# The product in three layer norms of a two-layer gated cross-attention block, made on VectorE instead of GpSimd

## The chip, the cores and the metric

The kernel runs on one core of one Trainium2 chip. The metric is the device time of one execution in microseconds (us), lower is better. It is given as the median of several executions.

## What is computed

The input `x` has 32 batches of 256 tokens with 256 features; `ctx` has 77 tokens for each batch. Two layers follow each other, each with a cross-attention and a feed-forward part. Each of the four parts begins with a layer norm and is added to the stream with a gate:

```
def _layernorm(x, axis=-1, eps=1e-05):
    m = jnp.mean(x, axis=axis, keepdims=True)
    v = jnp.var(x, axis=axis, keepdims=True)
    return (x - m) / jnp.sqrt(v + eps)

x = x + tanh(g_xattn[0]) * L0_xattn(_layernorm(x), ctx, ctx, mask, ...)   # relu attention        norm 0
x = x + tanh(g_ffn[0])   * L0_ffn(_layernorm(x), k0, k1, k2, s0, s1, s2)  # 256-1024-1024-256     norm 1
x = x + tanh(g_xattn[1]) * L1_xattn(_layernorm(x), ctx, Wq, Wkv, Wc)      # argmax, 16 heads      norm 2
x = x + tanh(g_ffn[1])   * L1_ffn(_layernorm(x), ...)                     # 64 experts, top 8     norm 3
```

## The kernel before

Everything is done batch by batch, and the engines run their instructions in an order that is written out by hand, one list for each engine, with semaphores between them. One round of the loop, `body(n)`, works on several batches at once: the second attention and the shared expert of batch c = n - 1, the first feed-forward of batch n, the first attention of batch m = n + 1, and GpSimd's scatters of batches n - 2 and n - 3. The round has two halves, `first(n)` and `second(n)`. Norms 1, 2 and 3 (the 2nd to 4th norm) lie in `second(n)`. Each core engine takes its own list strictly in order, so an instruction that waits holds all that stand behind it on its engine. After the 32 batches come the 64 experts, which the change does not touch.

A norm passes over four engines. VectorE makes the new stream tile (`a_x1`, L1529; `b_x2`, L1548; `c_x3`, L1618), its statistics (`ln_sums`, L1490) and from them `nt`, which holds the variance with EPS and the negated mean (`ln_moments`, L1502 and L1503, semaphore `ln_st`). GpSimd's `ln_coef(i, b)` makes the root `rs` = (variance + EPS) to the power -0.5 (L590) and the product `nb` = negated mean times `rs` (L592), and reports `ln_cf`. ScalarE's `ln_norm` (L726) waits for `ln_cf` and makes x * rs + nb. TensorE turns the result over (`transposes`, L986), ScalarE and VectorE take it out of PSUM in two halves (`tr_high`, L731; `tr_low`, L1512). Norm 0 is different: GpSimd normalises it itself (L601).

In `second(n)` the order on VectorE is: `c_x3` and the moments of norm 3, `b_l1(3)` (L1534), `a_x1` and the moments of norm 1, `tr_low(3)`, `b_x2` and the moments of norm 2, `d_gu(0)` (L1684 and L1686), `tr_low(1)`, `d_gu(1)`. On TensorE it is: half of the feed-forward's last product (`b_l2`, L1069), the transposes of norm 3, the other half, `d_gu(0)`, the transposes of norm 1, `d_gu(1)`, `d_route`, `d_gu(2)`, the transposes of norm 2. On GpSimd it is: `keep_x1` (L585), `ln_coef(3)`, a scatter, `ln_coef(1)`, two scatters, `ln_coef(2)`. A scatter is an indirect DMA issued by GpSimd (L574).

```
            def ln_norm(i, b, src, dst):              # ScalarE
                act.wait_ge(ln_cf[i], b + 1)
```

Of the kernel before, what the change touches and what calls it, by code (L numbers as in the profile page):

```python
# [13 lines left out]
ALU = mybir.AluOpType  # L14
# [78 lines left out]
def build(nc, x, ctxT, maskT, g_xattn, g_ffn, wq0, wk0, wv0, bq0, bk0, bv0, k0, k1, k2, s0, s1, s2,  # L93
          wqT1, wkvT1, wcT1, gates_w, sgu_w, sdown_w, egu_w, edown_w, out, xrows, table):
    es = ExitStack()
    with es:
        def sb(name, shape, dt=F32):
            return es.enter_context(nc.sbuf_tensor(name, shape, dt))
# [4 lines left out]
        def sems(name, n):  # L103
            return [sem(f"{name}{i}") for i in range(n)]
# [19 lines left out]
        def two(ap):  # L124
            return ap[:, :].rearrange("p (a n) -> p a n", a=2)
# [56 lines left out]
        nt = [sb(f"nt{i}", [P, 2, T2]) for i in range(4)]  # L182
        rs = [sb(f"rs{i}", [P, T2]) for i in range(4)]
        nb = [sb(f"nb{i}", [P, T2]) for i in range(4)]
# [95 lines left out]
        ln_st, ln_root, ln_cf, ln_nm, ln_dve = (sems(n, 4) for n in ("ln_st", "ln_root", "ln_cf", "ln_nm", "ln_dve"))  # L280
# [48 lines left out]
        def on(b):  # L329

            return not isinstance(b, int) or 0 <= b < NB
# [134 lines left out]
        def _(pool):  # L466
            g = nc.gpsimd
# [119 lines left out]
            def ln_coef(i, b):  # L587

                pool.wait_ge(ln_st[i], b + 1)
                g.tensor_tensor(rs[i][:, :], nt[i][:, 0, :], minushalf[:, :], ALU.pow).then_inc(ln_root[i], 1)  # L590
                pool.wait_ge(ln_root[i], b + 1)
                g.tensor_tensor(nb[i][:, :], nt[i][:, 1, :], rs[i][:, :], ALU.mult).then_inc(ln_cf[i], 1)  # L592

            def ln_norm(b):

# [8 lines left out]
            def body(n):  # L604
# [22 lines left out]
                if on(c):  # L627
                    ln_coef(3, c)
                if on(d):
                    scatter(d, 'c')  # L630
                if on(m):
                    ln_coef(1, m)
# [784 lines left out]
        def _(dve):  # L1417
            v = nc.vector
            ln_chain = [Steps(dve, ln_dve[i], 2) for i in range(4)]

            def plain(site):

                v.memset(dve_pad[:, site:site + 1], 0.0)
# [59 lines left out]
            def ln_sums(i, b, src, made, each=1):  # L1483


                w(dve, ln_nm[i], b)
                dve.wait_ge(made, each * b + each)
                ln_chain[i].start(b)
                for t in range(T2):
                    last = v.bn_stats(stats[i][:, t, :], src[:, t, :])  # L1490
                ln_chain[i].did(last)

            def ln_moments(i):

                ch = ln_chain[i]
                ch.wait()
                plain(8 + i)
                for t in range(T2):
                    last = v.bn_aggr(mv[i][:, t, :], stats[i][:, t, :])
                ch.did(last)  # L1500
                ch.wait()
                v.tensor_scalar(nt[i][:, 1, :], mv[i][:, :, 0], -1.0, None, ALU.mult)  # L1502
                v.tensor_scalar(nt[i][:, 0, :], mv[i][:, :, 1], EPS, None, ALU.add).then_inc(ln_st[i], 1)  # L1503
                ch.end()

            def ln_first(b):
                ln_sums(0, b, x0, x_in, 16)
                ln_moments(0)

            def tr_low(i, b, lo, hi):  # L1510
                dve.wait_ge(tr_hi[i], b + 1)
                v.tensor_tensor(lo[:, :, :], two(ps_turned[i]), hi[:, :, :], ALU.subtract).then_inc(tr_lo[i], 1)  # L1512


            def a_v(b):
                dve.wait_ge(v_rdy, b + 1)
                w(dve, vr_ev, b)
                v.scalar_tensor_tensor(v32[:, :], ps_pt0[0:S2, 0:D], 1 / WS, bv[0:S2, :], ALU.mult, ALU.add).then_inc(v_ev, 1)

            def a_l(b):  # L1520
                dve.wait_ge(s_ev, b + 1)
                w(dve, sv_rdy, b)
                v.tensor_tensor(l32[:, :], s32[:, :], mT[:, :], ALU.add).then_inc(l_ok, 1)

            def a_x1(b):
                dve.wait_ge(sv_ev, b + 1)
                w(dve, x1_copied, b)
                w(dve, ln_nm[1], b)
                v.scalar_tensor_tensor(x1[:, :, :], o32[:, :, :], G0X, x0[:, :, :], ALU.mult, ALU.add).then_inc(x1_ok, 1)  # L1529


            def b_lo(hi, lo, hh, hl, j, b):
                dve.wait_ge(hi.sem, hi.nth(j, b))
                v.scalar_tensor_tensor(hl[:, 2 * j:2 * j + 2, :], two(bank[j % 2]), 0.0, hh[:, 2 * j:2 * j + 2, :],  # L1534
                                       ALU.max, ALU.subtract).then_inc(lo.sem, 1)
# [4 lines left out]
            def b_l1(j, b):  # L1540
                b_lo(l1_hi, l1_lo, h1_h, h1_l, j, b)

            def b_x2(b):
                dve.wait_ge(l2_rdy, b + 1)
                dve.wait_ge(x1_copied, b + 1)
                w(dve, x3_ok, b)
                w(dve, ln_nm[2], b)
                v.scalar_tensor_tensor(x2[:, :, :], two(ps_yo), F0, x1_kept[:, :, :], ALU.mult, ALU.add).then_inc(x2_ok, 1)  # L1548
# [57 lines left out]
            def c_norm(r, b):  # L1606
                t, c = divmod(r, C2)
                dve.wait_ge(av_rdy.sem, av_rdy.nth(r, b))
                av = ps_m[:, 0:HC * VW].rearrange("p (h n) -> p h n", n=VW)
                v.reciprocal(rden[:, :], av[:, :, DH]).then_inc(av_dve, 1)  # L1610
                dve.wait_ge(av_dve, 5 * b + r + 2)
                v.tensor_tensor(att[:, t, c * P:(c + 1) * P].rearrange("p (h n) -> p h n", n=DH), av[:, :, 0:DH],
                                rden[:, :].unsqueeze(2).to_broadcast([P, HC, DH]), ALU.mult).then_inc(av_ev.sem, 1)

            def c_x3(b):
                dve.wait_ge(wc_rdy, b + 1)
                w(dve, x4_ok, b)
                v.scalar_tensor_tensor(x3[:, :, :], two(ps_m), G1X, x2[:, :, :], ALU.mult, ALU.add).then_inc(x3_ok, 1)  # L1618
# [61 lines left out]
            def d_gu(j, b):  # L1680

                dve.wait_ge(gu_th.sem, gu_th.nth(j, b))
                two_ = two(bank[j % 2])
                v.scalar_tensor_tensor(ga[:, j, :], th[:, j, :], 1.0, two_[:, 0, :], ALU.add, ALU.mult).then_inc(gu_dve, 1)  # L1684
                dve.wait_ge(gu_dve, 4 * b + j + 1)
                v.scalar_tensor_tensor(ac[:, j, :], ga[:, j, :], 0.5 / (WS * WS), two_[:, 1, :], ALU.mult, ALU.mult).then_inc(gu_ac.sem, 1)  # L1686

            def d_ac(j, b):
                dve.wait_ge(ac_hi.sem, ac_hi.nth(j, b))
                v.tensor_tensor(ac_l[:, j, :], ac[:, j, :], ac_h[:, j, :], ALU.subtract).then_inc(ac_lo.sem, 1)  # L1690
# [11 lines left out]
            def first(n):  # L1702
# [28 lines left out]
                if on(m) and on(n):  # L1731
                    ln_first(m)
# [28 lines left out]
            def second(n):  # L1761
                m, c = n + 1, n - 1
                if on(c):
                    c_norm(3, c)
                if on(n):
                    b_l1(1, n)
                if on(m):
                    a_v(m)
                if on(n):
                    b_l1(2, n)  # L1770
                if on(m):
                    a_l(m)
                if on(c):
                    tr_low(4, c, at_l, at_h)
                    c_x3(c)
                    ln_sums(3, c, x3, x3_ok)
                    ln_moments(3)
                if on(n):
                    b_l1(3, n)
                if on(m):  # L1780
                    a_x1(m)
                    ln_sums(1, m, x1, x1_ok)
                    ln_moments(1)
                if on(c):
                    tr_low(3, c, xt_l[3], xt_h[3])
                if on(n):
                    b_x2(n)
                    ln_sums(2, n, x2, x2_ok)
                    ln_moments(2)
                if on(c):  # L1790
                    d_gu(0, c)
                if on(m):
                    tr_low(1, m, xt_l[1], xt_h[1])
                if on(c):
                    d_gu(1, c)
                    d_gu(2, c)
                    d_ac(0, c)
# [5 lines left out]
            def last_batch(b):  # L1803
                c_norm(3, b)
                tr_low(4, b, at_l, at_h)
                c_x3(b)
                ln_sums(3, b, x3, x3_ok)
                ln_moments(3)
                tr_low(3, b, xt_l[3], xt_h[3])
                d_max(b)  # L1810
                d_gu(0, b)
                d_choose(b)
                d_gu(1, b)
                d_pos(b)
                d_slots(b)
                d_ac(0, b)
                d_ac(1, b)
                d_gu(2, b)
                d_gu(3, b)
                d_ac(2, b)  # L1820
                d_ac(3, b)
                d_x4(b)
# [124 lines left out]
```

## Time and profile before

| what | value |
|---|---|
| median of 3 runs | 1972.29 us (1964.68 to 1974.4) |
| time of the profiled execution | 1962.54 us |
| its span, first to last instruction | 1960.8 us |
| TensorE busy | 1706.9 us, 87% of the span |
| VectorE busy | 1329.0 us, 68% |
| GpSimd busy | 1068.3 us, 54% |
| ScalarE busy | 971.5 us, 50% |

The profile is of one execution. PE is TensorE's matmuls, DVE is VectorE, ACT is ScalarE, POOL is GpSimd. L592 is line 592 of the kernel. A row of the timeline gives the start, the duration, the engine, the line, the operation, the output and the inputs, and in brackets how long the engine had been idle and whose work ended that. Two VectorE rows can overlap by some tens of nanoseconds, since the next instruction starts before the last one's result is written. A transpose is a matmul on TensorE and appears as one.

### The profile page before, as it was taken

What the parts mean: (1) busy time and instruction counts of PE and PEld (TensorE: products, weight loads), DVE (VectorE), ACT (ScalarE), POOL (GpSimd) and SP (SyncE); (2) the same over time, 40 slices, a digit from 0 to 9 for tenths busy, and PEclk for the clock granted to TensorE, in tenths of its full rate; (3) what the DMA queues carried; (4) which work ended last, traced back from release to release, by engine and by line L of the source; (5) the groups of instructions that cost most, each with busy time, mean ns of one, the idle gap of its engine ahead of it and who ended that gap; (6) DMA issues with size and microseconds to landing.
All of it is one profiled execution on the core that took longest, in us unless ns stands there. A gap on an engine that the chain in (4) does not pass through costs nothing.

```text
span 1960.8 us, 51981 instructions
## 1 busy us (share of the span) xinstructions
PE 1706.9 (87%) x17309; PEld 1427.6 (73%) x17309; DVE 1329.0 (68%) x4615; ACT 971.5 (50%) x2803; POOL 1068.3 (54%) x1772
## 2 busy tenths in 40 slices
PE   3799999989899998999999999999999986457665
PEld 2687887878788887788878888888888864246554
DVE  5477777767677776677777777777777764335564
ACT  2365555555455554555555555555555543123332
POOL 2115555555455555555555555555555543568897
PEclk8899999999999999999999999999999997678999
DMA  4001100000000101000000000000000000147887
GB/s 126 8 14 21 21 19 19 19 14 19 19 19 19 19 19 19 19 19 19 17 16 19 19 19 19 19 19 19 19 19 19 18 13 13 45 124 186 199 205 154
DMA packets 97568, 80.15 MB, mean 41 GB/s; under 512 B 33835, under 2 KB 95224, under 8 KB 97528
## 3 DMA queue, kind: packets, MB, share of 16 engines
q1 hardware_dynamic: 68856, 60.46, 11.2%
q0 software_dynamic: 28672, 19.18, 5.5%
q8 instruction: 22, 0.36, 0.1%
q14 instruction: 18, 0.15, 0.0%
HBM read 51.63 MB, written 27.95 MB: 41 GB/s over the span
## 4 chain that ended last, share of the span: by engine, by line
PE 55%; issue 15%; DVE 14%; ACT 7%; POOL 4%; DMA 3%; another core or an unknown queue 1%; POOLq 0%; SPq 0%; DVEq 0%; ACTq 0%
PE bank L1055 15%; PE bank L964 7%; PE ps_m L964 5%; ACT p L787 3%; PE ps_lg L1113 3%; PE ps_yo L1069 3%; PE ps_lg L964 3%; PE ps_tr L986 3%; PE ps_yo L964 3%; PE ps_pt L1128 2%; PE bank L1041 2%; DMA xg<-xrows,gid 2%; PE ps_pt L964 1%; DVE rmax L1599 1%; PE ps_lg L1020 1%
## 5 line engine op out<-in xcount | busy, mean ns | idle before, releaser
L574 POOL DMA_INDIRECT table<-toki,slot x512 | 520.2, 1016 | 242.5 <-issue 196.3
L518 POOL TENSOR_TENSOR pool_pad<-pad_in 128x1 f32<-128x1 f32 x456 | 115.7, 254 | 400.8 <-PE ps_lg L1113 176.6
L787 ACT ACTIVATE p<-ps_lg,rmax 128x77 f32<-128x77 f32 x1024 | 235.6, 349 | 146.8 <-DVE rmax L1599 141.6
L1055 PE MATMUL bank<-h_h,wb 128*128 128x256 f16 x2048 | 266.3, 273 | 4.3 <-issue 2.2
L1055 PE MATMUL bank<-h_l,wb 128*128 128x256 f16 x2048 | 266.3, 273 | 0.0
L1055 PEld LDWEIGHTS bank<-h_l,wb 128*128 128x128 f16 x2048 | 200.8, 98 | 23.8 <-issue 0.2
L1055 PEld LDWEIGHTS bank<-h_h,wb 128*128 128x128 f16 x2048 | 193.2, 98 | 28.3 <-issue 2.8
L590 POOL TENSOR_TENSOR rs<-nt,minushalf 128x2 f32<-128x2 f32 x128 | 92.6, 724 | 188.2 <-DVE nt L1503 176.7
L1534 DVE SCALAR_TENSOR_TENSOR h_l<-bank,h_h 128x512 f16<-128x512 f32 x256 | 174.8, 683 | 12.0 <-ACT h_h L768 6.7
L1599 DVE TENSOR_REDUCE rmax<-ps_lg 128x8 f32<-128x616 f32 x128 | 101.6, 794 | 84.9 <-PE ps_lg L1113 84.8
L773 ACT ACTIVATE h_h<-bank 128x512 f16<-128x512 f32 x128 | 76.9, 601 | 124.3 <-PE bank L1055 124.3
L1512 DVE TENSOR_TENSOR xt_l<-ps_tr,xt_h 128x512 f16<-128x512 f32 x128 | 88.0, 687 | 62.9 <-ACT xt_h L731 52.3
L1069 PE MATMUL ps_yo<-wb,h_h 128*128 128x256 f16 x512 | 116.7, 275 | 0.1
L1069 PE MATMUL ps_yo<-wb,h_l 128*128 128x256 f16 x512 | 116.5, 274 | 0.0
L768 ACT ACTIVATE h_h<-bank 128x512 f16<-128x512 f32 x128 | 76.2, 597 | 80.6 <-PE bank L1041 44.3
L1604 DVE TENSOR_TENSOR pt_l<-ps_pt,pt_h 128x384 f16<-128x384 f32 x128 | 70.4, 550 | 65.7 <-ACT pt_h L793 65.5
L793 ACT ACTIVATE pt_h<-ps_pt 128x384 f16<-128x384 f32 x128 | 62.9, 491 | 103.4 <-PE ps_pt L1128 100.4
L680 POOL DMA_INDIRECT out<-ey,aid x64 | 101.5, 1586 | 18.6 <-POOL pool_pad L518 7.0
L964 PE MATMUL bank<-xt_h,gu_h 128*128 128x256 f16 x512 | 99.8, 277 | 10.6 <-DVE ac L1686 9.4
L1041 PE MATMUL bank<-xt_h,wb 128*128 128x256 f16 x512 | 100.0, 278 | 10.1 <-DVE dn_l L1438 5.9
L731 ACT ACTIVATE xt_h<-ps_tr 128x512 f16<-128x512 f32 x128 | 76.4, 597 | 60.2 <-PE ps_tr L986 53.0
L1490 DVE BATCH_NORM_STATS2 stats<-x 128x6 f32<-128x256 f32 x256 | 96.0, 417 | 13.4 <-DMA x<-in_x 3.7
(287 smaller groups left out, 4691.6 us busy)
## 6 DMA issues: line engine op xcount, KB each, us to landing
ew<-in_egu_w SPq DMA_DIRECT2D x64, 256.0 KB
xrows<-xr SPq DMA_DIRECT2D x32, 320.0 KB
x<-in_x SPq DMA_DIRECT2D x32, 256.0 KB
out<-x SPq DMA_DIRECT2D x32, 256.0 KB
table<-toki,slot POOLq DMA_INDIRECT x512
ew<-in_edown_w SPq DMA_DIRECT2D x64, 128.0 KB
ctx<-in_ctxT SPq DMA_DIRECT2D x32, 77.0 KB, 2.0
stage_b<-in_k SPq DMA_DIRECT2D x1, 1024.0 KB, 8.0
```

The source lines that it names most:

```text
L518: return g.tensor_tensor(pool_pad[:, site:site + 1], pad_in[:, :], pad_in[:, :], ALU.mult)
L574: g.indirect_dma_start(out=table, out_offset=bass.IndirectOffsetOnAxis(ap=slot[:, t, k:k + 1], axis=0), in_=toki[:, t:t + 1], in_offset=No ...
L590: g.tensor_tensor(rs[i][:, :], nt[i][:, 0, :], minushalf[:, :], ALU.pow).then_inc(ln_root[i], 1)
L680: g.indirect_dma_start(out=out, out_offset=bass.IndirectOffsetOnAxis(ap=aid[u][:, 0:1], axis=0), in_=ey[u][:, :], in_offset=None, bounds_c ...
L787: ins = a.activation(p32[:, h * S2:(h + 1) * S2], ps_lg[:, h // HB, h % HB * S2:(h % HB + 1) * S2], ACT.Exp, bias=rmax[r % 2][:, h:h + 1])
L964: ins = mm(out_, s_, m_, start=(start and i == 0), stop=(stop and i == len(seq) - 1))
L1041: ins = mm(two(bank[j % 2])[:, m % 2, :], s_, m_, start=(k == 0), stop=(k == 3))
L1055: ins = mm(two(bank[j % 2])[:, m % 2, :], wb1[:, k, m * P:(m + 1) * P], hp[:, k, :], start=(i == 0 and k == 0), stop=(i == 1 and k == FK - 1))
L1069: ins = mm(two(ps_yo)[:, t, :], hp[:, k, t * P:(t + 1) * P], wb2[:, k, :], start=(i == 0 and k == 0), stop=(i == 1 and k == FK - 1))
L1490: last = v.bn_stats(stats[i][:, t, :], src[:, t, :])
L1534: v.scalar_tensor_tensor(hl[:, 2 * j:2 * j + 2, :], two(bank[j % 2]), 0.0, hh[:, 2 * j:2 * j + 2, :], ALU.max, ALU.subtract).then_inc(lo.s ...
L1599: v.tensor_reduce(rmax[r % 2][:, :].rearrange("p (g h) -> p g h", g=2), lg, AX, ALU.max, negate=True).then_inc(z_ok.sem, 1)
```

## The change

For norms 1, 2 and 3 GpSimd makes only the root. A new VectorE function, `ln_shift`, waits for the root and makes the product. It stands one piece of work after the norm's moments: for norm 3 behind `b_l1(3)`, for norm 1 behind `tr_low(3)`, for norm 2 behind `d_gu(0)`. In the last batch it stands right behind the moments. Norm 0 stays on GpSimd.

```diff
@@ GpSimd, ln_coef
                 g.tensor_tensor(rs[i][:, :], nt[i][:, 0, :], minushalf[:, :], ALU.pow).then_inc(ln_root[i], 1)
-                pool.wait_ge(ln_root[i], b + 1)
-                g.tensor_tensor(nb[i][:, :], nt[i][:, 1, :], rs[i][:, :], ALU.mult).then_inc(ln_cf[i], 1)
+                if i == 0:
+                    pool.wait_ge(ln_root[i], b + 1)
+                    g.tensor_tensor(nb[i][:, :], nt[i][:, 1, :], rs[i][:, :], ALU.mult).then_inc(ln_cf[i], 1)
@@ VectorE
+            def ln_shift(i, b):
+                dve.wait_ge(ln_root[i], b + 1)
+                v.tensor_tensor(nb[i][:, :], nt[i][:, 1, :], rs[i][:, :], ALU.mult).then_inc(ln_cf[i], 1)
@@ VectorE, second(n)
                 if on(n):
                     b_l1(3, n)
+                if on(c):
+                    ln_shift(3, c)
                 if on(m):
                     a_x1(m)
                     ln_sums(1, m, x1, x1_ok)
                     ln_moments(1)
                 if on(c):
                     tr_low(3, c, xt_l[3], xt_h[3])
+                if on(m):
+                    ln_shift(1, m)
                 if on(n):
                     b_x2(n)
                     ln_sums(2, n, x2, x2_ok)
                     ln_moments(2)
                 if on(c):
                     d_gu(0, c)
+                if on(n):
+                    ln_shift(2, n)
                 if on(m):
                     tr_low(1, m, xt_l[1], xt_h[1])
@@ VectorE, last_batch(b)
                 ln_moments(3)
+                ln_shift(3, b)
                 tr_low(3, b, xt_l[3], xt_h[3])
```

## Rows read from the trace of the kernel before

**Rows 1.** The page: span, TensorE's busy time, its granted clock in 40 slices.

```profile
span 1960.8 us, 51981 instructions
PEclk8899999999999999999999999999999997678999
```

**Rows 2.** What TensorE waited for: us in total, times, longest.

```profile
PE ps_tr L986 <- ACT xr L726: 34.9, 25, 6.7
...
PE ps_tr L986 <- issue: 6.5, 6, 1.1
```

**Rows 3.** The chain that ended last, norm 3 of one batch: start, us.

```profile
828.28 0.73 POOL rs L590
...
829.09 0.58 POOL nb L592
...
829.78 1.10 ACT xr L726 x2
...
831.01 0.63 PE ps_tr L986 x4
```

**Rows 4.** Timeline of GpSimd, the same batch.

```profile
829.83 1.05 POOL L574 DMA_INDIRECT table<-toki,slot  x1 [0.17 <-issue]
831.12 0.72 POOL L590 TENSOR_TENSOR rs<-nt,minushalf 128x2 f32<-128x2 f32 x1 [0.24 <-DVE nt L1503]
...
835.67 0.72 POOL L590 TENSOR_TENSOR rs<-nt,minushalf 128x2 f32<-128x2 f32 x1 [0.73 <-DVE nt L1503]
```

**Rows 5.** Timeline of VectorE, the same batch.

```profile
828.11 0.68 DVE L1534 SCALAR_TENSOR_TENSOR h_l<-bank,h_h 128x512 f16<-128x512 f32 x1
828.86 0.75 DVE L1529 SCALAR_TENSOR_TENSOR x<-o,sc,x 128x512 f32<-128x512 f32 x1
...
830.86 0.16 DVE L1503 TENSOR_SCALAR nt<-mv 128x2 f32<-128x2 f32 x1
832.31 0.69 DVE L1512 TENSOR_TENSOR xt_l<-ps_tr,xt_h 128x512 f16<-128x512 f32 x1 [1.28 <-ACT xt_h L731]
833.42 0.75 DVE L1548 SCALAR_TENSOR_TENSOR x<-ps_yo,sc,x_kept 128x512 f32<-128x512 f32 x1 [0.43 <-PE ps_yo L1069]
...
835.94 0.42 DVE L1686 SCALAR_TENSOR_TENSOR ac<-ga,bank 128x256 f32<-128x256 f32 x1
```

**Rows 6.** Timeline of ScalarE, the same batch.

```profile
831.68 0.60 ACT L731 ACTIVATE xt_h<-ps_tr 128x512 f16<-128x512 f32 x1 [0.81 <-PE ps_tr L986]
832.17 1.08 ACT L726 ACTIVATE xn<-x,nb,rs 128x256 f32<-128x256 f32 x2
...
836.99 1.08 ACT L726 ACTIVATE xn<-x,nb,rs 128x256 f32<-128x256 f32 x2
```

**Rows 7.** Timeline of TensorE, the same batch: the transposes of norm 1.

```profile
834.53 0.60 PE L986 MATMUL ps_tr<-ident,xn 128*128 128x128 f32 x4
```

**Rows 8.** All products of GpSimd: durations min/median/max, then its group's busy us and mean ns.

```profile
L592 POOL TENSOR_TENSOR nb<-nt,rs x128: 193/196/609, 8.2 to 1681.0; 128x2 f32<-128x2 f32 x128
...
L592 POOL TENSOR_TENSOR nb<-nt,rs 128x2 f32<-128x2 f32 x128 | 35.4, 276 | 10.0
```

**Rows 9.** Groups of VectorE, by form.

```profile
L1588 DVE TENSOR_TENSOR vc<-vc 77x16 f16<-77x16 f32 x32 | 5.6, 175 | 1.1
...
L1668 DVE TENSOR_TENSOR val<-key,kept 128x128 f32<-128x128 f32 x32 | 9.4, 292 | 1.1
```

**Rows 10.** Timeline of GpSimd and VectorE, where VectorE waited for GpSimd.

```profile
523.90 0.62 POOL L585 COPY x_kept<-x 128x512 f32<-128x512 f32 x1
...
524.62 0.75 DVE L1529 SCALAR_TENSOR_TENSOR x<-o,sc,x 128x512 f32<-128x512 f32 x1 [5.78 <-POOL x_kept L585]
```

**Rows 11.** Timeline: a VectorE instruction with two SBUF inputs beside a scatter.

```profile
838.91 0.99 POOL L574 DMA_INDIRECT table<-toki,slot  x1 [0.45 <-issue]
...
839.37 0.42 DVE L1690 TENSOR_TENSOR ac_l<-ac,ac_h 128x256 f16<-128x256 f32 x1
```

**Rows 12.** Timeline of TensorE, norm 1 of a batch in which GpSimd's root came late.

```profile
1230.69 0.52 PE L986 MATMUL ps_tr<-ident,xn 128*128 128x128 f32 x3 [1.22 <-ACT xn L726]
```

## The prediction

> **What bounds the kernel now.** I read the page first: the span is 1960.8 us [rows 1], TensorE is busy in 87% of it (the table above), and its granted clock stands at 9 tenths or more of full speed in nearly every slice until the experts begin [rows 1]. So in the loop over the batches TensorE sets the pace, and the question is what keeps it idle there. The list of waits answers that. The longest wait of TensorE inside the loop is for `xr`, the output of norm 3, in front of the transposes of L986: 25 waits with 34.9 us, and six more of the same size whose releaser is given as issue, with 6.5 us [rows 2]. Without the longest (6.7 us, in a disturbed batch) and one of 4.6 us in the last batch, this is (34.9 - 6.7 - 4.6 + 6.5) / 29 = 1.04 us each. Batch by batch in the timeline it is nearly always 1.07 or 1.08 us. A batch takes 49.05 us from one `c_x3` to the next where nothing disturbs it, so this wait is 2% of the batch and the only gap of that size in it.
>
> Next I followed the chain of the last work through norm 3 of one batch [rows 3]. GpSimd's root runs from 828.28 for 0.73 us, to 829.01. The product starts at 829.09 and takes 0.58 us there. ScalarE starts at 829.78, and TensorE's transposes start at 831.01. All of it is on the path. The reader should see two things. From the end of the root to ScalarE's start 829.78 - 829.01 = 0.77 us go by. And the product of two numbers per partition takes far longer here than elsewhere: the median of all 128 is 196 ns [rows 8]. The group's busy time gives how often that happens: (35.4 - 128 x 0.196) / 0.39 = 26 products of about 0.59 us [rows 8], and the timeline shows that they are the ones of norm 3 in 26 of the 32 batches. In those batches VectorE's `a_x1` starts at 828.86 and runs until 829.61 [rows 5], and the product ends 0.05 us after it. In the batches where no `a_x1` runs beside the product it takes 0.20 us.
>
> **What the change does, part by part.** *Norm 3.* Removed from the path are the step from root to product (0.08), the product (0.58) and the step to ScalarE (0.11): 0.77 us [rows 3]. Put there are three terms. The step from GpSimd to VectorE: where VectorE did wait for GpSimd, `x_kept` ended at 523.90 + 0.62 = 524.52 and VectorE started at 524.62 [rows 10], so 0.10. The product on VectorE: the trace of before has none of this form. The nearest is a tensor_tensor of 16 elements with 0.175 us, and one of 128 elements takes 0.292 [rows 9]; I take 0.17, as it has only two elements. The step from VectorE to ScalarE: L1686 ended at 836.36 and ScalarE's next dependent instruction started at 836.40, so 0.04 (L1686 in [rows 5], ScalarE in the timeline). Sum 0.31, gain 0.77 - 0.31 = 0.46 us for each batch with a long product. Bounds: with 0.08, 0.15 and 0.03 for the terms the gain is 0.51; with 0.12, 0.29 and 0.05 it is 0.31.
>
> The wait is 1.07 us, so it stays above zero (0.61) and the gain is not cut off there. ScalarE is free: it had been idle for 0.95 us in front of this instruction.
>
> VectorE pays for it. It is free of `b_l1(3)` at 828.79 [rows 5] and now stands until 829.11. The product is followed by the next instruction 0.08 us after its start, as the two writers of `nt` are, so `a_x1` starts at about 829.19 instead of 828.86: 0.33 us later. What is queued behind the waiting instruction is `a_x1`, the moments of norm 1 and `tr_low(3)`. The moments ended at 831.02 and end at 831.35; VectorE then was idle for 1.28 us in front of `tr_low(3)` [rows 5]. That idle time hides the delay. `tr_low(3)` itself comes 0.46 us earlier with the transposes, at 831.85, still behind 831.35.
>
> *Norm 1.* Its product now stands behind `tr_low(3)`. The root is there by 831.35 + 0.10 + 0.72 = 832.17 (its length in [rows 4]). The product can start when `tr_low(3)` lets it, 831.85 + 0.61 = 832.46, so it doesn't wait. ScalarE starts `xn` at 832.46 + 0.17 + 0.04 = 832.67, against 832.17 before [rows 6], so 0.50 later. It ends at 833.75, and TensorE can have it at 833.88 with the same 0.13 as in [rows 3]. TensorE comes to these transposes at 834.53 [rows 7] minus 0.46, at 834.07. So 0.19 us are to spare, where it was 834.53 - 833.38 = 1.15. This cushion is thin: it is a fixed chain of 3.33 us behind the start of the transposes of norm 3 against 3.52 us of TensorE's own work (831.01 to 834.53). If the product takes 0.12 us more and waits for the end of `tr_low(3)`, nothing is left, and what is above that is lost in every batch.
>
> *Norm 2.* Its moments and its root are 0.46 us earlier with `b_x2`, which starts when TensorE lets it (VectorE idle 0.43 in front [rows 5]). GpSimd's root ends at 835.67 + 0.72 - 0.46 = 835.93 [rows 4]. GpSimd was idle for 0.73 us in front of it, so its two scatters don't hold it. VectorE is done with `d_gu(0)` at 836.36 - 0.46 = 835.90 [rows 5], waits until 836.03, and `nb` is there at 836.20. ScalarE takes up `xn` at 836.99 - 0.46 = 836.53, held by its own earlier work. So this product costs nothing and gives nothing. It delays `tr_low(1)` by some 0.3 us; the cover is the distance of 1.2 us to the transposes of norm 2, which need that buffer. Without the cover they would be 0.3 later.
>
> *GpSimd.* It has three instructions and waits less in each batch and issues the same scatters. It is idle in front of these roots, so its shorter list is worth nothing in itself. No queue of DMAs is passed over: no DMA moves.
>
> *Sum.* 26 batches by 0.46 = 12.0 us. In the other batches with a wait, and in the first and last ones, only a product of 0.20 us is replaced: (0.08 + 0.20 + 0.11) - 0.31 = 0.08, for some six of them 0.5 us. Everything behind the transposes of norm 3 (the next `c_x3` too) moves with them, as TensorE has no other gap of this size. Together -12.5 us: the profiled execution would be 1962.5 - 12.5 = 1950.0. Its own time is 9.8 us below the median of the runs, since some batches take 1 to 8 us more in any run. Against the median it is 1972.3 - 12.5 = 1959.8 us, or -0.63%.
>
> **A rule against the trace.** In the new order `a_x1`, which reads two SBUF tiles, starts at about 829.19, and GpSimd's scatter starts 0.17 us after it is free [rows 4], at 829.18. The row shows what such a pair did: the scatter of 838.91 with 0.99 us was under way when VectorE's L1690, with two SBUF inputs, started at 839.37, and this took its usual 0.42 us [rows 11]. So I cost `a_x1` at its 0.75 us. The Trainium skill (SBUF: State Buffer, section "SBUF: two separate sides") says that VectorE and GpSimd share a pair of ports with an exclusive lock, which a VectorE instruction with two SBUF inputs takes against a GpSimd instruction, and that the loser is blocked until the other has ended. By that rule the product of 0.58 us beside `a_x1` is a blocked one, and the trace agrees (0.196 where none runs beside it). By that rule a scatter that is first would hold `a_x1` too; [rows 11] speak against it, and what it would cost is the second rival below.
>
> **The rivals.** *The cushion of norm 1 gives way* (chance 0.14). If the step or the product is longer, the gain at norm 3 is 0.31, and the product at norm 1 eats a further 0.1 to 0.2. 26 x 0.15 = 4 us are left: 1968. For it: 0.19 us is little. Against it: all steps in it are read from rows.
>
> *The scatter holds `a_x1`* (0.06), the case on the other side. The place is 829.18, and it decides when the scatter is first. Its length is 1.05 us [rows 4], so `a_x1` starts 1.04 us later than forecast, the moments of norm 1 end at 831.35 + 1.04 = 832.39, the root at 833.21, the product at 833.21 + 0.10 + 0.17 = 833.48, ScalarE at 833.48 + 0.04 + 1.08 = 834.60, and TensorE starts at 834.73 instead of 834.53. Each batch is 0.20 longer, 26 x 0.20 = +5: 1977.
>
> *GpSimd's lateness reaches VectorE* (0.08). VectorE now waits for GpSimd three times a batch, with the whole stream queued behind. One batch shows what a late root costs: TensorE stood 1.22 us in front of norm 1 [rows 12], and that batch took 50.67 instead of 49.05. If it came in each of the 26 batches it would be +42 us; in a third of them +14, which takes back the gain: about 1974, and up to 2000. It decides from where GpSimd comes to norm 3 later by more than the 2.1 us for which it now stands idle in front of that root. Against it: only two of 30 batches show it, and the change takes work from GpSimd.
>
> *More than forecast* (0.05): the late batches become rarer too, 1954.
>
> **How the numbers follow.** The forecast has 0.67, the rivals 0.14, 0.06, 0.08 and 0.05. The three runs of before span 10 us, so a median of a few may be off by 3 to 4 us, and 0.5% (9.9 us), about what a measurement of this kernel can tell from no change, lies only 2.6 us from the forecast. Of the forecast's 0.67 I put 0.53 below 1962.4 and 0.14 above; with the last rival faster has 0.57. Within 0.5% are 0.14 of the forecast, 0.13 of the first rival, the second and some of the third, 0.36. Slower is 0.07. The likeliest case alone gives 1954 to 1966. The range reaches to the lower bound of 26 x 0.51 with a fast median, 1951, and above to the rivals at 1968 and 1974: 1975.
>
> **What would show it.** Norm 3's transposes wait 0.6 us instead of 1.07. The product on VectorE takes 0.17 us and starts 0.10 behind the root. `a_x1` starts 1.0 us after the moments of norm 3 instead of 0.66 and still takes 0.75. ScalarE's `xn` of norm 1 starts 0.5 us later and TensorE doesn't wait for it. A batch takes 48.6 us. I am wrong if TensorE waits in front of norm 1, if `a_x1` is longer, or if VectorE waits for GpSimd for more than 0.4 us in many batches.

## The result, and the profile after

The changed kernel took 1944.88 us, the median of four runs (1937.5 to 1945.69). The kernel before took 1968.49 us in four runs of the same time (1963.35 to 1974.4). The ratio is 0.9871, with a 95% interval of 0.9829 to 0.9912: 1.3% faster. The forecast was 1959.8 us, or 0.63% faster, with a range from 1951 to 1975, so the direction was right, the size half of what came, and the time lies below the range. The profiled execution took 1945.69 us with a span of 1944.0 us, against 1962.54 and 1960.8 before.

First the same view as in [rows 2], what TensorE waited for. Most lines have moved down by one, so L726 is L727 now and L986 is L987; those behind the moments on VectorE have moved by five (`b_l1` is L1539, `a_x1` L1534, `tr_low` L1517, `c_x3` L1623), and the product stands at L1509.

```profile
PE ps_tr L987 <- ACT xr L727: 23.0, 20, 7.1
...
PE ps_tr L987 <- issue: 6.0, 10, 0.6
```

The wait in front of norm 3's transposes was 34.9 + 6.5 = 41.4 us for 31 waits and is 23.0 + 6.0 = 29.0 for 30: 12.4 us less. Next the chain that ended last, through norm 3 of one undisturbed batch (start, us), beside [rows 3].

```profile
1412.00 0.73 POOL rs L590
...
1412.76 0.17 DVE nb L1509
...
1413.04 1.10 ACT xr L727 x2
...
1414.28 0.63 PE ps_tr L987 x4
```

From the end of the root to ScalarE's start it is 1413.04 - 1412.73 = 0.31 us, where it was 0.77. The timelines of the same batch follow, VectorE first, then GpSimd, ScalarE and TensorE (idle time in front of an instruction, with its releaser, in brackets).

```profile
1409.75 0.75 DVE L1623 SCALAR_TENSOR_TENSOR x<-ps_m,sc,x 128x512 f32<-128x512 f32 x1 [2.15 <-PE ps_m L965]
...
1411.83 0.68 DVE L1539 SCALAR_TENSOR_TENSOR h_l<-bank,h_h 128x512 f16<-128x512 f32 x1
1412.76 0.16 DVE L1509 TENSOR_TENSOR nb<-nt,rs 128x2 f32<-128x2 f32 x1 [0.25 <-POOL rs L590]
1412.88 0.76 DVE L1534 SCALAR_TENSOR_TENSOR x<-o,sc,x 128x512 f32<-128x512 f32 x1
...
1415.57 0.69 DVE L1517 TENSOR_TENSOR xt_l<-ps_tr,xt_h 128x512 f16<-128x512 f32 x1 [0.52 <-ACT xt_h L732]
1416.18 0.15 DVE L1509 TENSOR_TENSOR nb<-nt,rs 128x2 f32<-128x2 f32 x1
```

```profile
1412.92 1.05 POOL L574 DMA_INDIRECT table<-toki,slot  x1 [0.19 <-issue]
```

```profile
1413.04 1.09 ACT L727 ACTIVATE xr<-x,nb,rs 128x256 f32<-128x256 f32 x2 [0.49 <-DVE nb L1509]
...
1416.37 1.09 ACT L727 ACTIVATE xn<-x,nb,rs 128x256 f32<-128x256 f32 x2 [0.83 <-issue]
```

```profile
1408.92 0.38 PE L965 MATMUL ps_m<-wc_h,at_l 128*128 128x256 f16 x2
...
1414.28 0.63 PE L987 MATMUL ps_tr<-ident,xr 128*128 128x128 f32 x4 [0.61 <-ACT xr L727]
...
1417.80 0.60 PE L987 MATMUL ps_tr<-ident,xn 128*128 128x128 f32 x4
```

The reader should see that TensorE stands 0.61 us where it stood 1.07, that the product takes 0.16 us on VectorE, and that `a_x1` behind it takes its usual 0.76. TensorE doesn't wait in front of norm 1's transposes. An undisturbed batch, from one set of norm 3's transposes to the next, is 48.56 us where it was 49.05. Two things remain to be explained. The wait in front of norm 3 is 12.4 us shorter, but the time fell by 23.6. And before the experiments nothing said which of the product's two costs, its own length on GpSimd or `a_x1` beside it, had been in the way.

### The profile page after: what moved, and what is told of

Read it like the earlier page. It is cut to its first block, busy times and chain, and to the rows that moved or that the text cites. A ratio compares the mean times of both kernels' runs of the same rounds, so it can differ in the third digit from the quotient of the medians.

```text
span 1944.0 us, 51981 instructions
## 1 busy us (share of the span) xinstructions
PE 1708.6 (88%) x17309; PEld 1425.7 (73%) x17309; DVE 1340.3 (69%) x4711; ACT 974.4 (50%) x2803; POOL 1038.4 (53%) x1676
## 4 chain that ended last, share of the span: by engine, by line
PE 47%; issue 21%; DVE 13%; ACT 8%; POOL 7%; DMA 2%; another core or an unknown queue 1%; POOLq 1%; SPq 0%; DVEq 0%; ACTq 0%
PE bank L1056 13%; PE bank L965 8%; ACT p L788 4%; PE ps_yo L1070 3%; PE ps_lg L1114 3%; PE ps_tr L987 3%; PE ps_m L965 3%; PE ps_yo L965 3%; PE ps_pt L1129 2%; POOL table L574 2%; PE bank L1042 2%; POOL pool_pad L518 2%; DVE rmax L1604 2%; DVE pt_l L1609 1%; PE ps_lg L965 1%
## 5 line engine op out<-in xcount | busy, mean ns | idle before, releaser
L1056 PEld LDWEIGHTS bank<-h_h,wb 128*128 128x128 f16 x2048 | 193.4, 98 | 28.5 <-issue 2.9
L1539 DVE SCALAR_TENSOR_TENSOR h_l<-bank,h_h 128x512 f16<-128x512 f32 x256 | 175.0, 684 | 15.5 <-ACT h_h L769 10.6
L1517 DVE TENSOR_TENSOR xt_l<-ps_tr,xt_h 128x512 f16<-128x512 f32 x128 | 88.1, 688 | 35.8 <-ACT xt_h L732 28.6
```

What stands on the lines that cost most here:

```text
L1056: ins = mm(two(bank[j % 2])[:, m % 2, :], wb1[:, k, m * P:(m + 1) * P], hp[:, k, :], start=(i == 0 and k == 0), stop=(i == 1 and k == FK - 1))
```

## The experiments

There are four groups of kernels, and those of a group ran on one chip, together with the kernel before. The chips of the groups turned out not to be alike. Ratios are to the kernel before on the same chip, with 95% intervals. "Batch" is the time of an undisturbed batch.

### The two halves, and the wait alone

Four kernels: the change again, its norm 3 alone, its norms 1 and 2 alone, and the kernel before with `a_x1` held until GpSimd's product is done.

```diff
@@ r2_norm3, r3_norms12: which products stay on GpSimd (ln_shift only for the others)
-                if i == 0:
+                if i != 3:            # r2_norm3
+                if i in (0, 3):       # r3_norms12
@@ r4_alone: the kernel before, VectorE
                 if on(m):
+                    if on(c):
+                        dve.wait_ge(ln_cf[3], c + 1)
                     a_x1(m)
```

> The changed kernel once more, with more rounds. Theory A (all of the gain is the product of norm 3, 0.46 to 0.49 us in some 28 batches): -13.5 us, ratio 0.993. Theory B (something beside norm 3 gained too, as the first result suggests): -20 us or more, ratio 0.990 or less, and the profile's undisturbed batches still take 48.56 us, so that the rest must lie outside them.

> Only norm 3's product goes to VectorE; norms 1 and 2 keep theirs on GpSimd. Theory A: the whole gain, -13 us, batches of 48.5 us. Theory B (norms 1 and 2 or GpSimd's shorter list matter too): clearly less than the changed kernel gives, by a third or more.

> Only the products of norms 1 and 2 go to VectorE; norm 3's stays on GpSimd. Theory A: nothing, 49.05 us a batch, within 3 us of before. Theory B: a gain of 5 us or more.

> The kernel before, but a_x1 on VectorE waits for norm 3's product, so that the two don't run side by side. If a_x1 is what makes the product long: it takes 0.20 us instead of 0.59, ScalarE starts 0.39 earlier, a_x1 0.5 later, -10 us. If the product is long for another reason: it stays at 0.59, and the time is the same or up to 5 us longer.

Measured, against 1897.29 us of the kernel before (35 runs): r1_again 1892.81 us, ratio 0.997 [0.9947, 0.9994], batch 47.25 us. r2_norm3 1893.44, 0.9967 [0.9946, 0.9989], batch 47.22. r3_norms12 1895.05, 0.9991 [0.9964, 1.0018], batch 47.30. r4_alone 1899.78, 1.0016 [0.999, 1.0042], batch 47.30.

On this chip the kernel before is 3.6% faster than on the first, and the change is worth only 0.3%, or 0.05 us a batch. All four expectations rested on 49.05 us a batch and missed; of the times only r3_norms12's (within 3 us of before) came out. Below, a chip of the first kind is one like that of the first result (batches of 49.0 us), and one of the second kind is like this one. r4_alone can't tell here what `a_x1` beside the product costs, since the two don't meet on this chip in r3_norms12 either. The chain of r1_again shows what has taken the product's place, over norm 3 of one batch.

```profile
1374.54 0.88 PE ps_lg L1028 x4
...
1375.44 0.60 ACT o L763
...
1376.12 1.10 ACT xr L727 x2
...
1377.35 0.63 PE ps_tr L987 x4
```

Neither root nor product stands in it. ScalarE writes `o`, the output of `a_sv`, until 1376.04 and then goes straight on to `xr`. `c_x3` begins earlier here. The two lines below are the last product of `c_wc` on TensorE and the start of `c_x3` on VectorE in r1_again.

```profile
1372.41 0.38 PE L965 MATMUL ps_m<-wc_h,at_l 128*128 128x256 f16 x2
```

```profile
1372.83 0.75 DVE L1623 SCALAR_TENSOR_TENSOR x<-ps_m,sc,x 128x512 f32<-128x512 f32 x1 [1.74 <-PE ps_m L965]
```

VectorE starts 1372.83 - 1372.79 = 0.04 us behind TensorE's end. In the trace of the changed kernel above it was 1409.75 - 1409.30 = 0.45 us. The same code gives 0.04 in every batch of the four traces of this chip. In the first trace it gives 0.43 to 0.46 in 26 of the 32 batches, the same 26 in which the product is long, and 0.04 in the other six, in which it takes 0.20. ScalarE's start on norm 0's transposes differs in the same way (0.04 against some 0.3 us). So on this chip norm 3 is ready some 0.4 us sooner, while TensorE and ScalarE's `o` are where they were, and the product is hidden. The granted clock isn't the difference: from norm 3 of batch 19 to that of batch 29 it is 1.00 in all 18 traces. In r3_norms12 GpSimd's product takes only 0.19 us, with `a_x1` behind it instead of beside it:

```profile
1373.02 0.19 POOL L593 TENSOR_TENSOR nb<-nt,rs 128x2 f32<-128x2 f32 x1
```

### Norm 3 made later on purpose

If that is right, making `c_x3` late must bring the gain back. A memset on VectorE, expected at some 0.4 us and measured at 0.65, an addition to the work and nothing else, stands ahead of `c_x3`. It is put into the kernel before, the changed one and r4_alone. A plain copy of the kernel before shows which kind of chip this is.

```diff
@@ VectorE, c_x3
                 dve.wait_ge(wc_rdy, b + 1)
+                v.memset(late[:, :], 0.0)
                 w(dve, x4_ok, b)
```

> The kernel before itself, for its profile on the chip of these experiments and as a control: ratio 1.000. The four runs so far came from a chip on which undisturbed batches take 47.25 to 47.30 us, where c_x3 starts 0.04 us behind c_wc's last matmul; in the two traces of the first comparison it starts 0.45 behind it. If that is the chip and not the kernel: about 47.30 us a batch here, xr right behind ScalarE's output of a_sv, the product 0.20 us long and not beside a_x1, and a gap of TensorE of some 0.27 us. If it is the kernel before that is slow by itself: 47.7 us or more.

> The kernel before, with a memset of some 0.4 us on VectorE between the arrival of wc_rdy and c_x3, which puts norm 3 as late against ScalarE and a_x1 as in the first traces. Theory C (the gain of the change hangs on how late c_x3 comes): the product stretches to about 0.59 beside a_x1, TensorE's gap grows to some 1.07, a batch takes about 0.8 us more, +22 us. Theory D (lateness of c_x3 has nothing to do with it): less than +0.4 us a batch, +11.

> The changed kernel with the same memset. Theory C: 0.46 us a batch less than d1, about 13 us below d1, a gap of 0.6. Theory D: the same as d1 less the 0.05 us a batch of the kernels without it.

> r4 (product on GpSimd, a_x1 waits for it) with the same memset. If a_x1 beside it is what stretches the product: 0.20 instead of 0.59 us, 0.39 us a batch less than d1, 10 us below d1 and within 3 us of d2. If not: equal to d1 or slower.

Measured, against 1957.45 us of the kernel before (35 runs): b1_before 1956.86, ratio 1.0001 [0.9976, 1.0026]. d1_before_late 1965.42, 1.0048 [1.002, 1.0077], batch 49.40. d2_after_late 1953.11, 0.9982 [0.9956, 1.0008], batch 49.13. d3_alone_late 1960.02, 1.0026 [1.0003, 1.0049], batch 49.25. This chip is of the first kind (0.41 to 0.48 us in 26 batches of b1_before), so the memset made late what was late already, and `c_x3` behind it took 0.63 us instead of 0.75. So the question of this section, whether lateness alone brings the gain back on a chip of the second kind, wasn't put to the test, and d1_before_late's +22 us came out as +8. d2_after_late is 12.3 us below it, where 13 had been expected. But the three still tell the costs of the product apart. Below: d1_before_late (product, `a_x1`, TensorE's gap), then d3_alone_late, then d2_after_late.

```profile
1374.88 0.42 POOL L593 TENSOR_TENSOR nb<-nt,rs 128x2 f32<-128x2 f32 x1
...
1374.51 0.74 DVE L1530 SCALAR_TENSOR_TENSOR x<-o,sc,x 128x512 f32<-128x512 f32 x1
...
1376.65 0.63 PE L987 MATMUL ps_tr<-ident,xr 128*128 128x128 f32 x4 [1.39 <-ACT xr L727]
```

```profile
1370.76 0.19 POOL L593 TENSOR_TENSOR nb<-nt,rs 128x2 f32<-128x2 f32 x1
...
1370.99 0.75 DVE L1530 SCALAR_TENSOR_TENSOR x<-o,sc,x 128x512 f32<-128x512 f32 x1 [0.52 <-POOL nb L593]
...
1372.30 0.63 PE L987 MATMUL ps_tr<-ident,xr 128*128 128x128 f32 x4 [1.17 <-ACT xr L727]
```

```profile
1366.53 0.16 DVE L1510 TENSOR_TENSOR nb<-nt,rs 128x2 f32<-128x2 f32 x1 [0.25 <-POOL rs L591]
...
1368.05 0.63 PE L988 MATMUL ps_tr<-ident,xr 128*128 128x128 f32 x4 [1.09 <-ACT xr L728]
```

With `a_x1` beside it, GpSimd's product ends at 1375.30, 0.05 us behind the end of `a_x1` at 1374.51 + 0.74 = 1375.25, wherever it began: this time it lasts 0.42 us, in [rows 3] 0.58. With `a_x1` held back it takes 0.19, and TensorE's gap falls from 1.39 to 1.17. With the product on VectorE it falls to 1.09. So nearly three quarters of the gain in this gap, 0.22 of 0.30 us, come from `a_x1` no longer running beside the product, and the rest from the engine. Little more than half of it reaches the batch: 49.40 to 49.25 for the wait alone, against 49.13 for the change, or 0.15 of 0.27 us. In the times it is 5.4 of 12.3 us, where 10 us had been expected for d3_alone_late; what its later `a_x1` costs elsewhere wasn't traced. For the kernel before, where the product takes 0.59, an estimate of the same step in the gap is 0.59 - 0.19 = 0.40 of 0.46 us. No run shows it, as r4_alone ran on the other kind of chip only.

### The halves on a chip of the first kind, and a shorter product

r2_norm3 and r3_norms12 are repeated as a3_norm3 and a4_norms12, the change as a2_after. f1_fused is the changed kernel without the separate negation of the mean for norms 1 to 3; VectorE's product does it.

```diff
@@ f1_fused: VectorE, ln_moments and ln_shift
-                v.tensor_scalar(nt[i][:, 1, :], mv[i][:, :, 0], -1.0, None, ALU.mult)
+                if i == 0:
+                    v.tensor_scalar(nt[i][:, 1, :], mv[i][:, :, 0], -1.0, None, ALU.mult)
-                v.tensor_tensor(nb[i][:, :], nt[i][:, 1, :], rs[i][:, :], ALU.mult).then_inc(ln_cf[i], 1)
+                v.scalar_tensor_tensor(nb[i][:, :], mv[i][:, :, 0], -1.0, rs[i][:, :], ALU.mult, ALU.mult).then_inc(ln_cf[i], 1)
```

> The changed kernel a second time. On a chip where c_wc's signal reaches VectorE 0.45 us behind its last matmul (batches of 49.05 us before): theory C says -13.5 us, ratio 0.993, 48.56 us a batch. Theory E (the change also removes the batches of 49.7 us, in which the transposes of norm 0 reach ScalarE 0.7 us later; the kernel before showed 1 of 26 in one trace and 12 of 26 in another): up to 8 us more, ratio 0.989 to 0.993. On a chip with 0.04 us: ratio 0.997 again.

> Only norm 3's product on VectorE, as r2. With the 0.45 us signal: 48.55 us a batch, ratio within 0.002 of a2. With 0.04: as r2.

> Only the products of norms 1 and 2 on VectorE, as r3. With the 0.45 us signal: 49.05 us a batch, product of norm 3 still 0.59 us, ratio 1.000; theory E in its form that any shift of the order removes the 49.7 us batches: 0.997. With 0.04: as r3.

> The changed kernel without the separate negation of the mean: VectorE's product takes the mean itself times -1 times the root, in one instruction, so the variance is the first thing written and the root starts 0.07 to 0.08 us earlier. With the 0.45 us signal the gap of norm 3 shrinks by 0.07, 48.48 us a batch, 2 us below a2. With 0.04 nothing, since ScalarE's output of a_sv comes last there.

Measured, against 1958.1 us of the kernel before (17 runs): a2_after 1934.45, ratio 0.9873 [0.9845, 0.99], batch 48.53. a3_norm3 1937.77, 0.9896 [0.9869, 0.9923], batch 48.55. a4_norms12 1949.79, 0.996 [0.994, 0.9981], batch 49.00. f1_fused 1938.03, 0.9889 [0.9867, 0.9912], batch 48.37.

The first result is there again (0.9873 against 0.9871), so the 1.3% are no accident of four runs. Norm 3 alone has the whole gain per batch. Norms 1 and 2 alone leave the undisturbed batch as it was, and yet the kernel is 8 us faster. That is outside of what the sum knew. Norm 3 alone gives 20.3 us, of which its shorter gap makes 12.8 (28.5 us in its trace, against 41.3 in the mean of the four traces of before), so it too has 7 to 8 us besides; both halves together give 23.7, so what lies outside the gap doesn't add up from the halves. On the chip of the second kind norms 1 and 2 alone gave nothing that can be told from zero (0.9991). f1_fused shortens the batch by another 0.16 us, twice what was expected of the term that left the path (0.07 to 0.08); why twice wasn't traced. But its median doesn't tell it from a2_after, so it isn't shown to be a better kernel. Its profiled execution, 1952.92 us, was the slowest of its six. It had one batch of 59.97 us, and its experts took 291 us, together with a low granted clock, as the windows below show.

### How often a batch is 0.7 us longer

In 12 of the 26 batches from 3 to 28 of b1_before ScalarE took up norm 0's transposes 1.0 us behind their end, and TensorE stood some 0.70 us before it could go on to `d_cp` (L1207). Such a late batch takes 49.7 us and not 49.0 where nothing else disturbs it. One such batch of b1_before, TensorE, ScalarE, VectorE and TensorE again:

```profile
1404.58 0.60 PE L986 MATMUL ps_tr<-ident,xn 128*128 128x128 f32 x4
...
1406.19 0.60 ACT L731 ACTIVATE xt_h<-ps_tr 128x512 f16<-128x512 f32 x1 [0.87 <-PE ps_tr L986]
...
1406.82 0.69 DVE L1512 TENSOR_TENSOR xt_l<-ps_tr,xt_h 128x512 f16<-128x512 f32 x1 [0.85 <-ACT xt_h L731]
...
1407.57 0.23 PE L1207 MATMUL ps_tr<-chosen,before 128*128 128x64 f16 x2 [0.70 <-DVE xt_l L1512]
```

The transposes end at 1405.18 and ScalarE begins at 1406.19; in the other batches it begins 0.3 us behind. Of the other traces so far d1_before_late has 3 such waits and none of the others more than 2. Four more traces, of the same kernels as above, on one chip:

> The kernel before once more, for its trace. Counted are the batches from 3 to 28 in which ScalarE starts on norm 0's transposes over 0.6 us behind their end (12 of 26 in b1_before, 1 of 26 in the first trace). Theory E (late batches belong to the kernel before, and the change removes them: up to 8 us of the gain): 8 or more of 26 here, and in b3_before too. Rival (they fall in one execution and not in the next, whatever the kernel): 0 to 2 here in at least one of the two. Undisturbed batch 49.0 us by both, if the end of expert product to c_x3 is 0.45 us; 47.3 if it is 0.04.

> As b2_before, a third trace on the same chip. Theory E: 8 or more of 26 late batches in it too. Rival: a number that differs from b2_before's by more than 5, or is 0 to 2.

> The changed kernel once more on that chip. Theory E: 0 to 1 late batches of 26, span 20 us or more below the mean span of the two of before. Rival: some late batches in at least one of a5_after and a6_norms12, and a span lower by about 28 x 0.48 = 13 us. Undisturbed batch 48.55 us by both (47.25 if the signal comes after 0.04 us).

> Products of norms 1 and 2 alone on VectorE. Undisturbed batch 49.0 as before by both. Theory E: 0 to 1 late batches of 26, and a time some 8 us below before (ratio 0.996). Rival: late batches as often as in b2_before and b3_before, and no such difference.

Measured: b2_before 1971.04 us, b3_before 1958.46 and a5_after 1936.07, one run each; a6_norms12 1949.36 in ten runs, ratio 0.9964 [0.9938, 0.999]; the kernel before 1957.7 in 13. The list of waits counts the late batches by itself, TensorE at `d_cp` for `xt_l` (us in total, times, longest). First b1_before, then b2_before, then b3_before:

```profile
PE ps_tr L1207 <- DVE xt_l L1512: 9.0, 13, 0.7
```

```profile
PE ps_tr L1207 <- DVE xt_l L1512: 3.4, 5, 0.7
```

```profile
PE ps_tr L1207 <- DVE xt_l L1512: 3.5, 5, 0.7
```

The first trace of the kernel before has 1.4 us in 2. The list counts all batches; from 3 to 28 the kernel before has 1, 12, 5 and 4 late ones of 26, and over all batches 4.3 us of this wait in the mean. The changed kernel has 0, 1 and 0, and norms 1 and 2 alone 0 and 0. The expectation of 8 or more missed, and so did the rival's of 0 to 2 in one of the new traces of before. Theory E's 0 to 1 for a5_after and a6_norms12 held, and so did its times (a span 28.7 us below the mean of the two of before, and a ratio of 0.996). 22 of 104 against 1 of 130 is a difference, and it is worth about 4 us. But the late batches come in clusters by execution (12 in one, 1 in another), so these are four traces against five, and it isn't proof that the moved products do it: a3_norm3, d1_before_late and d3_alone_late keep GpSimd's products at norms 1 and 2 and have 0, 3 and 0, and f1_fused and d2_after_late without them have 1 and 0.

## Why the prediction was right in direction and too small

**The product on VectorE** was forecast at 0.10 + 0.17 + 0.04 us. It begins 0.03 behind the root (1412.73 to 1412.76), not 0.10, and takes 0.16. The step to ScalarE, 1412.92 to 1413.04, is 0.12 and not 0.04. So two terms were off by 0.07 and 0.08, in opposite directions, and the sum came out: 0.31 measured, 0.31 forecast, and the gain 0.46 at norm 3. The step of 0.10 had been read where a copy of 0.62 us ended [rows 10], which was not near enough in kind.

**TensorE's gap** was forecast at 0.61 us and is 0.61. **The batch** was forecast at 48.6 us and is 48.56.

**The lock** on the product beside `a_x1` was the right reading. With `a_x1` the product ends 0.05 us after it whatever its start, without it it takes 0.19 (d1_before_late, d3_alone_late). The Trainium skill (SBUF — State Buffer, section "SBUF: two separate sides") has this as an exclusive lock, whose loser waits for the other's end; the product's end agrees. The other side of it, that a GpSimd instruction which is first holds VectorE too, these rows don't bear out: GpSimd's root runs until 829.01 [rows 3] and `a_x1` starts at 828.86 [rows 5], while both take their usual 0.73 and 0.75 us. That such a lock would also let a scatter hold `a_x1` was the second rival. Here the scatter starts at 1412.92, 0.04 us after `a_x1`, so it is seldom first. In the one batch of each of the three traces of the changed kernel in which it was, by 0.07 to 0.09 us, `a_x1` took 0.75 us. The rival is refuted as far as three cases go.

**Norm 1's cushion** was forecast at 0.19 us. `xn` ends at 1416.37 + 1.09 = 1417.46, TensorE could have it 0.13 later, at 1417.59, and comes to it at 1417.80: 0.21. It held. **GpSimd's lateness** didn't reach VectorE: in 26 batches of each trace VectorE waits 0.25 us for the root.

**Where it failed** is the step from norm 3 to the whole kernel: "Everything behind the transposes of norm 3 [...] moves with them, as TensorE has no other gap of this size", and so "Together -12.5". The term that it summed was right. Over the 31 batches behind the first, TensorE's gap in front of norm 3 fell from 41.3 us (mean of four traces of the kernel before) to 28.8 (mean of three of the changed one), by 12.6 us; 12.2 of them are the 26 batches with a long product, by 0.47 each. What it put at nothing is all else that differs between the two kernels' executions, 11.8 us; the late batches it had only as a rival with a chance of 0.05, at 1954 us. The table sets the stretches of the four traces of before (the first, b1, b2, b3) beside the three of the changed kernel (the first, a2, a5), means in us, cut at norm 3's transposes.

| stretch | before | after | difference |
|---|---|---|---|
| start to the first | 121.6 | 120.4 | -1.2 |
| batches 2 to 9 | 406.0 | 401.8 | -4.2 |
| batches 10 to 29 | 994.6 | 981.8 | -12.8 |
| batches 30 to 32 | 159.7 | 157.9 | -1.8 |
| from the last on | 279.8 | 275.4 | -4.4 |
| span | 1961.6 | 1937.2 | -24.4 |

Of the 24.4 us, 12.6 are norm 3's gap. The late batches are a second part, 4.3 - 0.2 = 4 us. A third, 4.4 us, is the experts' stretch at the end, which the change doesn't touch. The rest, some 3 us, is 1.2 in the stretch ahead of the first norm 3 and some 2 in other waits of the batches, of which some are shorter and some longer; they weren't followed further. The experts' stretch varies from 273 to 291 us over all traces, longer where the granted clock is lower. The windows from the last norm 3 on show it (us, busy time and count of PE, PEld, DVE, ACT and POOL, then the granted clock, the DMA share and GB/s): b2_before, a5_after and f1_fused.

```profile
1681.00:1968.00 287.00, 180.72 (x1114) 150.80 (x1114) 138.37 (x562) 76.69 (x205) 217.76 (x261) 0.85 0.65 156
```

```profile
1660.00:1933.00 273.00, 168.11 (x1114) 138.20 (x1114) 141.31 (x562) 76.86 (x204) 217.97 (x260) 0.91 0.67 164
```

```profile
1660.00:1950.00 290.00, 184.99 (x1114) 154.82 (x1114) 138.98 (x562) 76.75 (x205) 217.51 (x260) 0.83 0.64 154
```

The same 1114 instructions take TensorE 168 us at a mean granted clock of 0.91 and 185 at 0.83. Between the two levels of 2.4 and 1.2 GHz a mean of 0.83 is the higher one with (1 - 0.83) / 0.5 = a third of the stretch at the lower, and 0.91 with a fifth. In this stretch TensorE stops again and again for the experts' tokens, as the list of waits of the changed kernel has it:

```profile
PE ps_tr L1366 <- DMA xg<-xrows,gid: 36.5, 30, 4.6
PE ps_m L1366 <- DMA xg<-xrows,gid: 34.3, 31, 3.1
```

Whether the changed kernel gets the higher clock by right or the four and three traces drew it by chance isn't settled: its traces have 0.92, 0.91 and 0.91, those of before 0.89, 0.91, 0.85 and 0.87, a3_norm3 0.90, a4_norms12 0.89 and a6_norms12 0.91. So of 24 us, between 12 and 13 are shown step by step and are what was forecast, about 4 are the late batches, seen often before and seldom after but without a shown cause, and the other 8, the experts' stretch above all, may be chance. That the total came out at twice the forecast is thus open for its second half, though the 1.3% themselves came twice.

**The chip** is the other thing that the forecast left out. That the gain hangs on which of `o` and the root comes last was in the profile. In the changed kernel ScalarE waits 0.49 us between `o` and `xr`; before it waited 0.95, as the prediction says. The forecast used this as room for ScalarE and didn't ask what would happen if norm 3 came 0.4 us sooner.

## What to carry to other kernels

A tiny instruction of GpSimd on the path is priced by what VectorE runs beside it: ask first whether the neighbour can start later, since the wait alone had most of the gain in the gap here, and then what the delayed neighbour costs, since only about half of the gain reached the batch and the time. When a gap has two feeders (here the root by way of the product, and ScalarE's earlier output), write down the slack of the second; it says how much of the gain survives when the first comes sooner for another reason, as on the other chip. And when a gain is sized, split several traces of both kernels into the same stretches: the undisturbed batch told the mechanism within 0.01 us from one trace, while three and four traces weren't enough to tell the stretches with varying waits and clock from chance. Multiply such a gain by the batches that have the gap, counted in the trace, and not by all.

## What the runs showed of the hardware that was not expected

The same program takes 1897 us in one group, on one chip, and 1957 to 1968 in the four other measurements, of the result and of three groups; its undisturbed batches are 47.3 us on the one (GpSimd's product at norm 3 still in place, in r3_norms12 and r4_alone) and 49.0 us in the others. At the level of instructions the difference shows at a few handovers from TensorE: VectorE or ScalarE begins 0.04 us behind the modelled end of the matmuls on the one and 0.3 to 0.45 on the other, at `c_wc`, norm 0's transposes and the argmax. The memset of the d kernels stands right behind the wait for `c_wc` and began 0.56 to 0.65 us behind in 26 batches and 0.21 to 0.26 in the others, so it is this wait that ends late and none of the others of `c_x3`. The trace also holds the times at which semaphores were raised, and they say on whose side the delay lies. TensorE's semaphore for `c_wc` goes up 0.01 us behind the modelled end in r1_again and 0.40 to 0.45 behind it in 26 batches of the first two traces. That of norm 0's transposes goes up 0.01 us behind against 0.25 to 0.29 in nearly all batches, or 0.98 to 1.00 in the late ones of b1_before. `c_x3` on VectorE and ScalarE's instruction start 0.02 to 0.03 us after it each time. So TensorE or its signal is late, not the engine that waits. For `c_wc` it is the same 26 batches in all 14 traces of the first kind. In them GpSimd's `x_kept` (L585) has begun 0.04 to 0.06 us ahead of `c_wc`'s end, and in the six others it hasn't; but in r1_again it has begun as early and nothing is late, so this alone isn't the cause. Why only at these places, why on some chips, and why now and then 1.0 us, stays open; no experiment here tried it.
